# Feed forward of a gated cross-attention block: the second layer follows the first by one step in place of two

## The reference, cut to what matters

```python
h = layernorm(layernorm(x)) * ln_gamma + ln_beta      # rows of 512
w1 = dequant(fc1_q, fc1_scales)                       # 512 x 2048, one scale per 128 rows
y  = silu(h @ w1 + fc1_bias)
w2 = dequant(fc2_q, fc2_scales)                       # 2048 x 512
z  = y @ w2 + fc2_bias
x  = x + tanh(g_ffn) * (layernorm(x) + 0.5 * z)
```

## Time and profile before

| | us |
|---|---|
| median of 3 runs | 3076.88 |
| lowest, highest | 3070.58, 3080.24 |
| the profiled execution | 3075.3 |
| its span | 3073.5 |

### The profile page before, as it was taken

One profiled execution on the slowest core, in us unless ns is written; L12 is line 12 of the kernel. 1 busy time (PEld: TensorE's weight loads), 2 busy tenths in 40 slices (PEclk: granted clock), 3 DMA queues, 4 the chain that ended last, 5 costly groups with the idle time before them and its releaser, 6 DMA issues. The chain is left out here.

```text
span 3073.5 us, 50982 instructions
## 1 busy us (share of the span) xinstructions
PE 2954.7 (96%) x14950; PEld 1787.7 (58%) x14950; DVE 2163.4 (70%) x3166; ACT 1629.9 (53%) x2961; POOL 1831.1 (60%) x880
## 2 busy tenths in 40 slices
PE   7999979999999999999999999999978799999999
PEld 6888754444444444444444444444447477777777
DVE  5554557777777777777777777777757787777775
ACT  3222226666666666666666666666621444444443
POOL 4655638888888888888888888888833000000000
PEclk9999979999999999999999999999989899999999
DMA  6666752222222212221222222122159200000000
GB/s 208 226 223 230 230 197 59 47 62 62 51 53 62 61 44 61 62 57 46 62 62 50 54 62 61 43 62 62 47 132 277 109 28 28 28 28 14 22 20 28
DMA packets 145488, 255.25 MB, mean 83 GB/s; under 512 B 22066, under 2 KB 64114, under 8 KB 138228
## 3 DMA queue, kind: packets, MB, share of 16 engines
q1 hardware_dynamic: 145396, 254.13, 29.3%
HBM read 162.32 MB, written 91.23 MB: 82 GB/s over the span
## 5 line engine op out<-in xcount | busy, mean ns | idle before, releaser
L918 DVE TENSOR_REDUCE at_half_max<-ps 128x1 f32<-128x1024 f32 x1024 | 1217.0, 1220 | 458.3 <-PE ps L718 452.6
L718 PE MATMUL ps<-k_stack,q_stack 96*128 96x512 f32 x2048 | 706.6, 427 | 15.5 <-issue 11.7
L863 ACT ACTIVATE probT<-ps 128x512 f32<-128x512 f32 x1024 | 536.6, 603 | 229.3 <-PE ps L737 229.2
L737 PE MATMUL ps<-q_stack,k_stack 98*128 98x512 f32 x2048 | 656.3, 401 | 1.3 <-ACT probT L863 1.0
L863 ACT ACTIVATE at_probT<-ps 128x512 f32<-128x512 f32 x1024 | 536.3, 603 | 222.0 <-PE ps L737 222.0
L718 PEld LDWEIGHTS ps<-k_stack,q_stack 96*128 96x128 f32 x2048 | 349.3, 191 | 492.4 <-issue 325.4
L604 POOL TENSOR_TENSOR at_gp_sum<-at_gp_sum,probT 128x1024 f32<-128x1024 f32 x256 | 609.9, 2382 | 21.5 <-POOL at_gp_sum L604 0.4
L604 POOL TENSOR_TENSOR at_gp_sum<-at_gp_sum,at_probT 128x1024 f32<-128x1024 f32 x256 | 608.7, 2378 | 21.1
L737 PEld LDWEIGHTS ps<-q_stack,k_stack 98*128 98x128 f32 x2048 | 385.0, 188 | 173.9 <-ACT probT L863 52.8
L1478 POOL TENSOR_TENSOR x_keep<-x_keep,b_half 128x2048 f32<-128x2048 f32 x8 | 37.5, 4684 | 546.9 <-DVE x_keep L1501 546.9
L1531 DVE SCALAR_TENSOR_TENSOR ff_acc<-ps,s_t,ff_acc 128x512 f32<-128x512 f32 x384 | 288.2, 750 | 20.6 <-DVE ff_acc L1531 0.5
(11 more groups left out here) (195 smaller groups left out, 3880.1 us busy)
## 6 DMA issues: line engine op xcount, KB each, us to landing
k_stack<-kT_hi SPq DMA_DIRECT2D x128, 256.0 KB, 5.0
kT_hi<-pi_out_hi SPq DMA_DIRECT2D x16, 1024.0 KB, 4.4
kT_lo<-pi_out_lo SPq DMA_DIRECT2D x16, 1024.0 KB, 6.7
v_heads<-pi_v_out SPq DMA_DIRECT2D x16, 1024.0 KB, 10.5
q_stack<-qT_hi SPq DMA_DIRECT2D x128, 128.0 KB, 3.4
k_stack<-kT_lo SPq DMA_DIRECT2D x64, 256.0 KB, 4.3
v_head<-v_heads SPq DMA_DIRECT2D x64, 256.0 KB, 5.1
pi_c_in<-in_ctx_dram SPq DMA_DIRECT2D x16, 768.0 KB, 9.8
```

The lines of the kernel that those rows point to most:

```text
L718: mm = pe.matmul(ps[:, n, :], q_stack[buf][0:PARTS, rows], k_stack[buf][0:PARTS, BANK * n:BANK * (n + 1)], start=True, stop=True)
L737: pe.matmul(ps[:, key_bank(lane, kv), :], k_stack[buf][0:rows, P * kv:P * (kv + 1)], q_stack[buf][0:rows, q:q + BANK], start=True, stop=Tr ...
L863: act.activation(probT[lane % 2][:, kv, :], src, ACT.Exp).then_inc(exp_done, 1)
L918: dve.tensor_reduce(dst, src, AX_X, ALU.max).then_inc(max_done, 1)
```

## The change

One constant of `feed_forward` is changed.

```diff
@@ -1290,7 +1290,7 @@
     CH = R // TT
     UNROLL = 2 * FT
     STEPS = CH * FT
-    LAG = 2
+    LAG = 1
     GROUP = 4
     W2_AHEAD = 3
```

## The result

The changed kernel takes 3091.59 us, the median of 6 runs (3089.02 to 3093.05), against 3075.86 for the kernel before in the same comparison. The ratio is 1.0056, with a 95% interval of 1.0043 to 1.0068. It is 15.7 us slower. The span of its profiled execution is 3091.3 us, 17.8 more than before.

A forecast was written before the change was run, and what follows sets the result against it. PE was taken as the bound, busy 2954.7 of 3073.5 us. The terms 12.4+4.5-1.2=+15.7 us on the profiled execution's 3075.3 gave 3091.0 us, with a range of 3079 to 3100.

The forecast's parts named there:

- place 2: Slots 10 and 11, chunks 1 to 6: POOL's bias addition holds y_lo(9), for which PE now waits directly; +4.5 us net.
- chunk 0: First chunk, while fc2 is restored: second(0) moves into a gap, 0 us; up to 1.5 us kept for the range.
- Plain steps: Steps without extra work: slack falls to 0.56 us in the loop and 0.36 outside, so no cost and no gain.
- Place 1: End of a chunk, 7 boundaries: evictions ahead of y_lo(0) on DVE leave PE waiting, 1.77 us each, +12.4 us.
- The term of the clock: Behind the unbroken stalls in slot 10: PE's clock drops in five chunks of six, 1.56 us each, 7.8 us.
- Rival B: PE's clock stays up in the long stalls of slot 10: 7.8 us less, 3083.2 us; chance 0.08.
- Rival A: Slots 9 and 10: DVE takes the port before POOL, so y_lo(9) takes 0.68 us; -11.4 us, 3063.9 us; chance 0.09.
- The end, -1.2: End of the kernel: second(127) starts when y_lo is there and ends at T+9.06, before at T+10.24; -1.2 us.

## Why the prediction was right

The forecast was 3091.0 us and +15.7; measured were 3091.6 and +15.7. The agreement to a tenth is luck: the interval of the ratio stands for 13 to 21 us, and the forecast was added up from profile rows, where the two spans differ by 17.8. There the boundaries came out 1.3 us too low, place 2 by 0.8 and chunk 0 by 0.8, and an earlier start, outside the change, took 0.9 back. What was right is the mechanism. The profile shows which steps carried it.

- *Plain steps cost nothing*: right, they stand at 4.66 us. The chain is even 0.12 us shorter than taken. Acc starts at T+0.67 in place of T+0.79 (2666.49 from T0 2665.82), since ACT is not held by the wait of y_hi any more and is ready before PE. The prediction saw that wait go, and missed that acc had stood behind it.
- *Place 1*: right in mechanism. 1.8 to 1.9 us a boundary against 1.77: in the loop PE begins 0.13 us behind the end of y_lo, not 0.03 (2674.14 against 2673.33+0.68), and outside it 0.06, so a hand-over between ACT and DVE was the wrong row for one from DVE to PE. The term that was mis-sized most is one boundary of 2.5 us: the way back of the loop on DVE, 0.6 us, which the slack of LAG 2 had covered. No row that the prediction read showed it, though the trace of before has it: y_lo(15) of chunk 3 starts 1.47 us behind the start of y_hi there, in place of 0.67. 13.7 in all against 12.4. And the delay was not "hidden wholly" before: it cost 1.8 us in slot 10 of chunks 1 and 6, which the prediction counted under POOL. The sum is the same either way.
- *Place 2*: the stall in one piece is 3.38 us in the loop and 3.58 outside against 3.51 and 3.69: the chain is 0.12 us shorter and POOL's addition 0.07 (4.53 against 4.60), less a few hundredths in PE's restart. The term of the clock was 7.8 us for five drops and came out at 30.1-4x3.38-2x3.58=9.4 for four. The number was too high and the size too small: in three chunks the clock stayed at half for 6.8 us, and there it cost 2.5 to 2.8, not 1.56. The two errors offset each other. Rival B is out in this profile, but in the three other kernels with the same stall the clock fell in two, two and six of the six chunks, so this term is a matter of the execution.
- *Rival A* didn't come, with POOL ahead by the 0.05 us that the rows of before gave, six times of six; brought about on purpose, it gave its time. The rule in the Trainium skill's "SBUF — State Buffer" (SBUF: two separate sides), that who starts first keeps the other out for the whole instruction, agrees with the traces: y_lo lasts 5.03 or 5.04 us behind a POOL that is 0.04 us ahead, and 0.68 where it is first. The cast, which no row of before showed against POOL, was held too, 2.41 us, though it has one input in SBUF and the rule as the prediction tells it speaks of two.
- *Chunk 0 at 0*: 0.8 us too low, inside the 1.5 kept for it. Acc(2) waited 0.82 us for PE behind a second(0) at half clock, and counted from first(0), y_hi was 0.8 later than before from slot 4 to slot 10. As first(0) began 0.9 us earlier in that profile, it doesn't show in the sum.
- *The end, -1.2*: measured -1.2.

What stays open: what decides whether and when the clock falls at such a stall. How long it then stays low went with the moment of the fall. In the four kernels with the stall it fell 14 times in 24. In six cases it fell 0.70 to 1.24 us before PE went on, as at 2718.83 with PE going on at 2719.96, and stayed at half for 6.8 us. In the other eight it fell at most 0.55 us before PE went on, or after that, and stayed for 3.4 us. No run set this moment on purpose.

## What to carry to other kernels

The distance between a producer's step and its consumer's is a store of slack, and on an engine without gaps it earns nothing to spend it: less distance gave back 1.2 us at the end and cost 14 where one engine does extra work once a chunk. Before such a change look for everything that holds the producers for longer than the new slack, once a chunk and not only in plain steps, and for stalls that are paid already. And where one engine's long instruction holds another's short one by being 0.05 us ahead, a wait sets them apart: with LAG 2, making POOL wait for DVE's instruction won 22 us, and four small pieces with such waits won 28.

## What the runs showed that was not expected

- The way back to the start of a loop of 32 steps held DVE's next instruction until 2.52 us after the one before, 1.16 more than y_hi's wait does there (1.36), and cost PE 0.6 us once the slack was gone.
- A stall of PE of one size (3.4 to 3.6 us) was met by full clock, by 3.4 us or by 6.8 us at the 1.2 GHz level, in one and the same execution.
- In chunks 1 to 6 a POOL addition of 512 columns took 1.29 or 1.30 us, and beside the sums it didn't hold DVE, where one of 2048 took 4.52 to 4.64 and held a y_lo or a cast each time.
- A delay of 1.7 us at the start of a chunk, hidden by the slack of the second layer, came out seven slots later at the transposes, where the chain made up only 0.1 us a step.
